# GpSimd's indirect sends of places 2 to 7 without their waits for the tensor engine's transposes

## What is computed

```python
x = x + _L0_xattn_ref(_layernorm(x), fside_BxS2xS2_0, ctx_1024)      # quantised two-layer expert
x = x + _L0_ffn_ref(_layernorm(x), lut, gate_idx, up_idx, down_idx)  # weights picked from a table
x = x + _L1_xattn_ref(ctx_1024, _layernorm(x), ...)                  # state-space scan
x = x + _L1_ffn_ref(_layernorm(x), gate_w, w_gate, w_up, w_down)     # 32 experts, top 8 of 32
# _L1_ffn_ref, per batch of rows:
#   probs = softmax(x @ gate_w); w, sel = top_k(probs, 8)
#   xg[e] = the rows whose choice holds expert e
#   y = (silu(xg @ w_gate[e]) * (xg @ w_up[e])) @ w_down[e]
#   out[row] += weight * y
```

## Time and profile before

| | |
|---|---|
| median of 3 runs | 1835.95 us (1835.48 to 1837.2) |
| the profiled execution | 1838.54 us |
| its span, first to last instruction | 1836.8 us |
| mean granted clock of PE | 0.905 of 2.4 GHz |
| PE busy with matmuls | 1548.2 us, 84% |
| VectorE, ScalarE, GpSimd busy | 71%, 50%, 43% |
| mean rate of all DMAs | 243 GB/s |

### The profile page before, as it was taken

How to read it: one execution, slowest core, us unless ns; L and a number is a source line. 1 busy time by engine, 2 the same in 40 slices (tenths; PEclk the granted TensorE clock), 3 DMA queues, 4 the chain that set the end, 5 groups by cost and what they waited for, 6 DMA issues and landing times. The chain is left out here.

```text
span 1836.8 us, 26417 instructions
## 1 busy us (share of the span) xinstructions
PE 1548.2 (84%) x9418; PEld 1317.3 (72%) x9426; DVE 1312.9 (71%) x1901; ACT 910.5 (50%) x1577; POOL 798.9 (43%) x485
## 2 busy tenths in 40 slices
PE   5866768678638986997799689978999999999896
PEld 4444455445438986896799679857888898989795
DVE  6776588775769989998999999744555555555452
ACT  3444544536344445344444534424666666665563
POOL 1010010010055456545679557556515676762545
PEclk9878878888769996998799789989999999999998
DMA  7988889986873491376169437759989999999876
GB/s 205 345 261 274 283 313 366 324 299 199 300 267 105 172 358 60 137 264 259 65 222 385 198 112 247 268 190 349 357 289 245 254 257 262 260 246 233 217 176 83
DMA packets 189014, 445.87 MB, mean 243 GB/s; under 512 B 42688, under 2 KB 44736, under 8 KB 178640
## 3 DMA queue, kind: packets, MB, share of 16 engines
q1 hardware_dynamic: 116112, 283.76, 46.0%
q0 software_dynamic: 31760, 74.48, 17.3%
q10 hardware_dynamic: 41008, 85.89, 13.0%
HBM read 246.97 MB, written 205.48 MB: 246 GB/s over the span
## 5 line engine op out<-in xcount | busy, mean ns | idle before, releaser
L1535 POOL TENSOR_TENSOR mix_st<-mix_Bb,mix_du 128x2048 f32<-128x2048 f32 x64 | 293.4, 4584 | 227.8 <-DVE mix_st L2398 208.3
L2390 DVE TENSOR_TENSOR_SCAN mix_st<-mix_YY,mix_st 128x512 f32<-128x512 f32 x256 | 311.8, 1218 | 35.0 <-ACT mix_YY L2055 34.7
L2055 ACT ACTIVATE mix_YY<-mix_dt,mix_A 128x512 f32<-128x512 f32 x256 | 177.0, 691 | 285.7 <-DVE mix_st L2390 285.4
L1614 POOL DMA_INDIRECT out_x<-moe_ys,moe_meta x130 | 207.8, 1599 | 198.1 <-ACT moe_ys L2203 120.1
L1747 PE MATMUL mix_G<-mix_xThi,mix_wup 128*128 128x256 f32 x1408 | 273.1, 291 | 16.9 <-issue 16.2
L1747 PEld LDWEIGHTS mix_G<-mix_xThi,mix_wup 128*128 128x128 f32 x1408 | 231.7, 199 | 19.7 <-issue 18.1
L1954 PE MATMUL mix_Dp<-moe_xhi,moe_whi 128*128 128x288 f32 x768 | 233.0, 303 | 1.5 <-ACT moe_xhi L2166 1.5
L1954 PE MATMUL mix_Dp<-moe_xlo,moe_whi 128*128 128x288 f32 x768 | 227.3, 296 | 0.0
L1954 PE MATMUL mix_Dp<-moe_xhi,moe_wlo 128*128 128x288 f32 x768 | 227.2, 296 | 0.0
L458 PE MATMUL front_L<-front_oh,front_pick 128*128 128x512 f32 x528 | 178.1, 475 | 45.2 <-ACT front_wst L605 28.8
L1773 PE MATMUL mix_YY<-mix_ident,mix_st 128*128 128x128 f32 x1024 | 148.7, 301 | 69.7 <-DVE mix_st L2398 69.7
(11 more groups left out here) (260 smaller groups left out, 3057.8 us busy)
## 6 DMA issues: line engine op xcount, KB each, us to landing
x_by_expert<-front_zeros ACTq DMA_DIRECT2D x16, 4480.0 KB, 24.5
mix_wup<-w_halves SPq DMA_DIRECT2D x44, 1024.0 KB, 5.6
moe_raw<-in_ew SPq DMA_DIRECT2D x32, 1280.0 KB, 8.1
moe_xt<-x_by_expert SPq DMA_DIRECT2D x128, 256.0 KB, 7.8
mix_wdn<-w_halves SPq DMA_DIRECT2D x44, 512.0 KB, 7.1
front_idx<-in_idx SPq DMA_DIRECT2D x44, 384.0 KB, 9.1
w_halves<-front_wst SPq DMA_DIRECT2D x44, 384.0 KB, 8.1
mix_Bb<-bc_rows SPq DMA_DIRECT2D x16, 1024.0 KB, 10.5
```

What stands on the lines that cost most here:

```text
L1535: nc.gpsimd.tensor_tensor(st[:, g % STBUF, :, :], Bb[:, q, :, :], du[:, k % 2, :].unsqueeze(1).to_broadcast([P, NG, S]), ALU.mult).then_in ...
L1614: pool.indirect_dma_start(out=out_rows, out_offset=bass.IndirectOffsetOnAxis(ap=meta[0:rows, e % MBUF, j, 0:1].bitcast(U32), axis=0), in_= ...
L2055: nc.scalar.activation(dA, dt[:, k % 2, :], ACT.Exp, scale=A[:, c, m:m + 1]).then_inc(da_ready, 1)
L2390: nc.vector.tensor_tensor_scan(r, dA, r, 0.0, ALU.mult, ALU.add).then_inc(scanned, 1)
```

## The change

POOL no longer waits for PE's transposes between the places. `sends_on_chip`, `sends`, their order, their number and every other wait stay as they are.

```diff
             sends(EARLY, 0)
             sends(EARLY + 1, 0)
             for k in range(1, TOP):
-                if k > 1:
-                    pool.wait_ge(e_xT_ready, NT * (k - 2) + 2)
                 sends_on_chip(k)
                 sends(EARLY, k)
                 sends(EARLY + 1, k)
```

## The result

The changed kernel takes 1839.79 us (median of 12 executions, 1835.92 to 1846.85) against 1835.28 us of the kernel before in the same rounds (12 executions, 1832.18 to 1839.45). The ratio is 1.0024 with a 95% interval of 1.0013 to 1.0036: slower, by about 4.5 us. I had forecast 1 us less. The time is inside the range, but on the other side of it, in the case that I gave 17%.

What follows compares the result with a forecast made beforehand. The prediction took PE's pace and its 5.8 us of tile-load waits to bound the kernel. Its terms, -1.0 us at (6, 3) and 0 elsewhere, gave 1835.95 - 1.0 = 1835.0 us, range 1833.6 to 1840.5.

Steps and rivals of the forecast that it cites:

- What bounds the kernel: PE's two tile-load waits, 5.8 us from 1256 to 1400 us; the 4.78 us one costs 7.45 us with the clock.
- The removed waits and the dates: Six POOL waits go, 17.8 us; last send near 1316.2, expert 6's loads 3.5 to 8.5 us earlier.
- The first wait, (2, 2): PE's 4.78 us wait for expert 2's third tile: grows 0 to 1.0 us, costing 0 to 1.6; taken as 0.
- The second wait, (6, 3): PE's 0.99 us wait for a tile of expert 6: disappears because its loads start earlier, -1.0 us.
- Experts 3, 4 and 5: Their tile loads show no PE wait and were to get none beside the unbroken sends; booked 0.
- The rule of turns between queues: DMA engines go round queues a packet at a time, so POOL's queue length leaves SP's turn unchanged; supported booking 0.
- rows 9 and 10: Profile rows of tile landings: expert 3, 11.2 to 14.2 us after issue; expert 4, up to 14.5 us.
- rival A: Nothing gained, as full DMAs delay loads by what earlier sends win; 1835.95 to 1835.95 + 1.6, say 1836.5; chance 0.20.
- B: Rival: unpaused sends starve tile loads of experts 4 to 6; 1840 to 1845, say 1842; chance 0.17.
- its mark of about 18 us for expert 4: Landing time of expert 4's loads at which B decides; each microsecond beyond costs 1 to 1.56 us.

Runs made afterwards that it cites:

- e10: Kernel before with weights of experts 2 to 9 issued behind tiles 2, 3 and 4 in SP's order, POOL's waits kept: 1831.72 us, ratio 0.997.
- e1: The changed kernel once more, unaltered, on another measurement against the kernel before: 1843.18 us, ratio 1.0038.
- e2: Kernel before with only POOL's waits before places 2 and 3 removed: 1836.72 us, ratio 0.9998.
- e3: Kernel before with only POOL's waits before places 5 to 7 removed: 1841.24 us, ratio 1.003.
- e9: Changed kernel with a small POOL computation behind every third send of places 3 to 7: 1836.64 us, ratio 0.9999.
- e5: Changed kernel with a small POOL computation behind every third send of places 3 to 7, on the slow chip: 1863.59 us, ratio 0.9957.
- e8: Changed kernel loading one eighth of the weights of experts 2 to 7, on the slow chip: 1908.86 us, ratio 1.0196.
- e6: Kernel before with weights of experts 2 to 9 issued behind tiles 2, 3 and 4, POOL's waits kept, slow chip: 1872.29 us, ratio 0.9993.
- e7: Changed kernel with weights of experts 2 to 9 issued behind tiles 2, 3 and 4, on the slow chip: 1908.21 us, ratio 1.0194.

## Why the prediction was wrong

*What bounds the kernel.* Right: PE's waits for tiles, with the price of the clock. When the load of (2, 2) was really brought forward, in e10, 5.6 us came back, with a new wait of 3.0 us for weights against it, where I had priced its wait at 7.45.

*The removed waits and the dates.* Right for POOL: last send forecast near 1316.2, measured 1315.16. The loads of expert 5 and 6 were to start at 1302.7 to 1306.1 and 1318.8 to 1323.8. They started at 1298.67 and 1309.86. Some 2 us of that is the earlier start of the experts in this execution; in e1, which starts as before, they are 1299.79 and 1313.28, with the last send at 1316.40. So the sends landed sooner than I allowed. That is already the sign of what I missed: they got more of the DMAs than I had given them, and someone else got less.

*The first wait, (2, 2).* I took 0 out of 0 to 1.0 us. Measured 5.68, 4.33, and 3.54 in e2, against 4.78: it moves by about 1 us either way between executions, and e2's time shows no cost.

*The second wait, (6, 3).* Right in the profile after: gone.

*Experts 3, 4 and 5.* This is the step that failed: "So a tile lands as late behind a short queue of sends as behind a long one, and I book 0." In place of that 0 the profiles have 2.1 us of waits at expert 5 in the first one and 6.8 us at experts 4 and 5 in e1, and the times 4.5 and 7.2 us. I rested the 0 on expert 3, whose tiles land in 11.2 to 14.2 us, and called the stretch from 1270.60 to 1286.50 in the earlier trace rows unbroken. It is not: it has 7 sends in 15.90 us, where a send every 1.28 us makes 12, and POOL stood 7.34 us before the send at 1287.02. Half of the flight of expert 3's loads fell into that pause. In the changed kernel the stream goes on. There the three tiles behind the weights land in up to 14.2 us for expert 3, up to 15.1 for expert 4 and up to 21.6 for expert 5: one expert shows nothing yet, and the loads' backlog adds up from expert to expert.

What counts is not how many sends wait but how many bytes the sends take per us, and for how long. I had every number for that sum. With sends at 0.287 MB per 1.28 us, 224 GB/s, and the 402 GB/s of the earlier trace rows, 178 GB/s are left. An expert's 1.31 MB of weights, 1.18 MB of tiles and, in the first six, 1.18 MB of stored results are 3.67 MB, or 20.6 us at that rate, where PE needs 17.6. With the 172 GB/s of sends before, 230 are left, and the same bytes take 16.0 us. Three experts in a row, 3, 4 and 5, run into the 3 us that are missing before the stream ends. That makes 9 us by this estimate, and the middle one of expert 5's three tiles behind the weights lands 8 us later after its issue than before (20.4 for 12.4). The pauses before places 5, 6 and 7 were what gave the loads their share, as e3 and e9 show.

The rule of turns between queues, which the prediction cites from the Trainium skill ("DMA: Bandwidth & Descriptors", section "Queues, rings and completion order") as saying the same as rows 9 and 10, was read into too much. That the length of a queue does not change a turn may well hold; no run here shows it. It says nothing of how many turns a queue takes in all. A stream with pauses leaves some to the others, which would fit the 229 GB/s of sends for 172, but that is argued and not tested. The same skill's sentence about issuing from several engines ("Trainium Kernel Development and Optimization", section "Key Constraints"), on which rival A stood, comes nearer to the result: earlier issue brought no time. The loss it does not tell.

*The rivals.* B came true in its main point: loads behind the weights come late beside an unbroken stream. Its price is nearly right (1840 to 1845 forecast, 1839.79 and 1843.18 measured). Its place is so in part. I had set its mark of about 18 us for expert 4, whose tiles stayed below it (15.1) and hardly made PE wait (0.2 us in e1). It was expert 5 that went beyond (20.4 to 21.6), and expert 6, whose tiles behind the weights were issued after the stream's end, had no wait. And B blamed the number of sends that wait, where the sum above goes by their rate. I gave it 17% because of one row. The sum would have spoken for it.

## What to carry to other kernels

When a wait on one queue is removed, add up what all queues must move in one turn of the bounding engine, and take the freed queue at its full rate: if the rest no longer fits into the turn, the wait may have been a share of bandwidth for the others, as it was here. One load that lands in time beside a stream proves nothing for the third in a row. And where an engine waits for a small load, look first at what is ahead of it in its own queue: 1.3 MB that nobody needed yet stood before the tiles, and moving it behind them was worth more than any change to the other queue tried here.

## What the runs showed of the hardware

e5 to e8 ran on a chip where the kernel before takes 1873.19 us (17 executions, 1867.28 to 1875.35), some 37 us more than in the other measurements, and there the order of the kernels is another one.

| on that chip | median us | ratio | 95% interval |
|---|---|---|---|
| e5, a pause behind every third send | 1863.59 | 0.9957 | 0.9941 to 0.9973 |
| e6, weights behind, waits kept | 1872.29 | 0.9993 | 0.9981 to 1.0006 |
| e7, weights behind, no waits | 1908.21 | 1.0194 | 1.0176 to 1.0212 |
| e8, no waits, light weights | 1908.86 | 1.0196 | 1.0177 to 1.0214 |

In e7's profile ScalarE, VectorE, TensorE and SyncE all but stop while the sends run. Three stretches and ScalarE in order of time:

```profile
1270.00:1280.00 10.00, 0.00 (x0) 0.00 (x0) 0.00 (x0) 0.00 (x0) 7.57 (x9) 0.50 0.56 220
1280.00:1290.00 10.00, 0.00 (x0) 0.00 (x0) 0.00 (x0) 0.00 (x0) 7.56 (x9) 0.50 0.57 228
...
1320.00:1330.00 10.00, 6.94 (x29) 5.52 (x28) 6.54 (x11) 7.09 (x14) 0.00 (x0) 0.74 0.13 41
```
```profile
1263.55 0.60 ACT L2167 ACTIVATE moe_xhi<-mix_G 128x512 fp32r<-128x512 f32 x1 [10.79 <-remote]
1308.35 0.38 ACT L2167 ACTIVATE moe_xhi<-mix_G 128x256 fp32r<-128x256 f32 x1 [44.20 <-remote]
```

Between 1270 and 1290 us only POOL works, and the DMAs move little but the sends' own 224 GB/s. TensorE waits for VectorE, and the waits of VectorE and ScalarE end on nothing that the profile shows ("remote", "issue"). SyncE's two tile loads from 1263.54 on take 45.13 us to issue. TensorE takes up at 1309.33, shortly before the last send (1311.73), and ScalarE and VectorE work steadily again only from 1322.4 on. In e8 it is the same, with light weights (229 and 228 GB/s in the same two stretches), so on that chip contention of bytes doesn't explain it. In e5, whose stream has short pauses from place 3 on, the longest wait of PE in this part is 21.7 us; in e7 it is 54.5 us. What the engines lack there, their instructions or their semaphores, no run here tells, and it stays open. So does whether the kernel before loses its 37 us in the same way, since I have no profile of it from that chip. What can be said is that an unbroken stream of GpSimd's indirect DMAs cost 35 us there (e7 and e8 against the kernel before) and 3 to 7 us elsewhere, and that, for the same loads, the kernels with pauses were the faster ones on both kinds of chip.
